# A transformer block on one core: residual and bias put in the output by transfers, a bitwise-or in the search, and the first expert made ready in the context stage

## What is computed

```
xn = (x - mean) / sqrt(var + 1e-5)
q, k, v = split(xn @ W_qkv + b_qkv);  16 heads of 32;  q, k = relu(q), relu(k)
kv_cos = sum over l of (k * cos_l) v;  kv_sin the same with sin_l      (per batch and head)
context = (q cos_l) kv_cos + (q sin_l) kv_sin;  norm the same with the sums of k
attn = (context / (norm + 1e-4)) @ W_out + b_out
probs = softmax(xn @ choice_w.T);  each of 8 experts takes the 1024 rows of a batch with its highest probs
ffn[row] += prob * (silu(xn[row] @ w1[e]) @ w2[e])
out = x + attn + ffn
```

## Time and profile before

| | us |
|---|---|
| median of 3 runs | 2571.82 (2569.92 to 2573.37) |
| the profiled execution | 2573.36 |
| its span in the profile | 2571.6 |
| TensorE busy | 2449.5 (95%) |
| VectorE busy | 1436.1 (56%) |
| GpSimd busy | 1101.0 (43%) |
| ScalarE busy | 664.8 (26%) |
| mean granted clock | 0.98 |

### The profile page before, as it was taken

The page is one execution under the profiler, slowest core; times in us unless marked ns, Lnnn a source line. Parts: engine busy times, 40 slices in busy tenths (PEclk is TensorE's granted clock), DMA queues, the critical chain, the costliest instruction groups (busy, mean ns, idle before and its releaser), DMA issues.

```text
span 2571.6 us, 38730 instructions
## 1 busy us (share of the span) xinstructions
PE 2449.5 (95%) x12990; PEld 2074.7 (81%) x12990; DVE 1436.1 (56%) x3019; ACT 664.8 (26%) x1108; POOL 1101.0 (43%) x938
## 2 busy tenths in 40 slices
PE   6999989999999889769999999999999999999997
PEld 5999978879999878658878878888788788788786
DVE  6666669976666689843444354443534534543443
ACT  3222223322222233222232222322322322322222
POOL 0000015410000055366656566575666666565665
PEclk9999989999999999879999999999999999999999
DMA  5111012321111233243252242433342432522522
GB/s 157 61 37 65 33 43 94 102 90 40 57 49 49 70 113 100 72 101 52 44 115 48 46 112 45 78 81 51 75 83 48 107 52 42 115 48 45 113 45 42
DMA packets 106797, 181.63 MB, mean 71 GB/s; under 512 B 31761, under 2 KB 31761, under 8 KB 106769
## 3 DMA queue, kind: packets, MB, share of 16 engines
q0 software_dynamic: 39552, 68.75, 15.1%
q1 hardware_dynamic: 67216, 112.57, 14.3%
HBM read 112.83 MB, written 68.42 MB: 70 GB/s over the span
## 4 chain that ended last, share of the span: by engine, by line
PE 79%; DVE 12%; issue 4%; DVEq 1%; DMA 1%; POOL 1%; ACT 1%; SPq 1%; POOLq 0%; ACTq 0%
PE ps L1030 26%; PE ps L1031 26%; PE ps L1032 26%; DVE thr L776 2%; DVE work L849 2%; DVE xo L877 1%; DVE k_lo L865 1%; DVE one_lo L916 1%; PE ps L1046 1%; DVE mark L766 1%; DVE w_lo L1003 1%; PE ps L1199 1%; POOL rows L428 1%; DVE rden L853 1%; DVE rden L855 1%
## 5 line engine op out<-in xcount | busy, mean ns | idle before, releaser
L428 POOL DMA_INDIRECT rows<-normed_rows,idx_row x528 | 565.8, 1072 | 207.9 <-issue 206.7
L1030 PE MATMUL ps<-xi_hi,w_hi 128*128 128x512 f32 x1024 | 406.3, 397 | 27.0 <-DVE xi_lo L960 27.0
L1031 PE MATMUL ps<-xi_lo,w_hi 128*128 128x512 f32 x1024 | 400.8, 391 | 0.0
L1030 PE MATMUL ps<-w_hi,h_hi 128*128 128x512 f32 x1024 | 400.2, 391 | 0.0
L1032 PE MATMUL ps<-xi_hi,w_lo 128*128 128x512 f32 x1024 | 399.5, 390 | 0.0
L1032 PE MATMUL ps<-w_hi,h_lo 128*128 128x512 f32 x1024 | 398.8, 389 | 0.0
L1031 PE MATMUL ps<-w_lo,h_hi 128*128 128x512 f32 x1024 | 398.4, 389 | 0.0
L407 POOL TENSOR_TENSOR vv_lo<-qT,vv_hi 128x512 fp32r<-128x512 f32 x64 | 83.4, 1304 | 729.8 <-ACT vv_hi L536 729.7
L997 DVE CAST h_hi<-hf 128x512 fp32r<-128x512 f32 x256 | 111.1, 434 | 441.5 <-ACT hf L580 438.5
L473 POOL DMA_INDIRECT out_dram<-y,idx x128 | 224.6, 1754 | 294.9 <-ACT y L599 278.0
L580 ACT ACTIVATE hf<-ps 128x512 f32<-128x512 f32 x256 | 153.1, 598 | 538.6 <-PE ps L1032 538.6
(11 more groups left out here) (157 smaller groups left out, 4440.9 us busy)
## 6 DMA issues: line engine op xcount, KB each, us to landing
w_raw<-in_L_ffn_w_dram SPq DMA_DIRECT2D x36, 512.0 KB, 8.4
w_raw<-in_L_ffn_w_dram SPq DMA_DIRECT2D x9, 2048.0 KB
xo<-in_L_attn_x_dram SPq DMA_DIRECT2D x34, 512.0 KB, 3.9
normed_rows<-xn SPq DMA_DIRECT2D x34, 512.0 KB, 3.0
xo<-in_L_attn_x_dram SPq DMA_DIRECT2D x64, 256.0 KB, 2.6
out_dram<-xo SPq DMA_DIRECT2D x64, 256.0 KB, 2.0
rows<-normed_rows,idx_row POOLq DMA_INDIRECT x528, 2.6
qT<-in_L_attn_W_qkv_dram SPq DMA_DIRECT2D x3, 1024.0 KB, 8.1
```

Source lines behind the costliest of these rows:

```text
L428: nc.gpsimd.indirect_dma_start(rows[:, tt, a, :], None, pieces[:, :], bass.IndirectOffsetOnAxis(ap=idx_row[:, b, first_tile + tt, a:a + 1] ...
L1030: nc.tensor.matmul(dst, a_hi, b_hi, start=start, stop=False, skip_group_check=True)
L1031: nc.tensor.matmul(dst, a_hi, b_lo, start=False, stop=False, skip_group_check=True)
```

## The change

- **Output.** At the start of each batch GpSimd's queue copies x to the output from DRAM to DRAM, 1024 rows a transfer, and adds the bias by an accumulating transfer from a broadcast tile. In the context stage ScalarE copies the output product to `xo`, and GpSimd stores it with an accumulating transfer. The loads of x, GpSimd's sum, VectorE's sum and SP's stores go.
- **Search.** `settle` multiplies the comparison with the bit's pattern and ors it into the threshold; no predicated copy. The search runs one step earlier: TensorE's count for bit t-1 comes between context products and transposes of step t.
- **Last block of a batch.** Its q products 1 to 3 come behind the last `kv`. In batch 0 the normalised rows of the next batch are turned in step 32 of the context stage; in the last batch nothing is normalised ahead.
- **First expert.** In the context stage of batch 1, list, gather (one transfer a step, steps 11 to 30), transposes, xi, the high part of w1 and half of its remainder are made. w1 is loaded when the projection is done, w2 when the last tile of q is split.
- **Lists in the experts** are made behind up products 4 to 7 in place of 3 to 6.
- **Start.** `choice_w` is loaded by one transfer and transposed by TensorE; w_out is split by GpSimd alone; ScalarE copies q product 0 before the square root.
- The loops over batches and over context steps are written out.

```diff
+            sp.dma_start(ch_rows, choice_w[:, :]).then_inc(ch_in, 16)
...
-                for k in range(KD):
-                    sp.dma_start(ch[:, k, :], choice_w[:, k * P:(k + 1) * P].rearrange("e p -> p e")
-                                 ).then_inc(con_in, 16)
...
+                if b == B - 1:
+
+                    sp.wait_ge(mm_done, AHEAD + B * NBLK * 12)
+                    load_w1(0)
+                    sp.wait_ge(q_ready, B * NT)
+                    load_w2(0)
...
-            pool.wait_ge(w_hi_ready, 4)
+            pool.wait_ge(w_in[O], 16)
+            nc.gpsimd.tensor_copy(wo_hi[:, :, :], raw_weights(O)).then_inc(wo_hi_ready, 1)
+            pool.wait_ge(wo_hi_ready, 1)
...
+            def first_rows(t):
+
+                if t == 10:
+                    for s in range(2):
+                        pool.wait_ge(xn_stored[s], 16 * B * NBLK)
+                    pool.wait_ge(prob_stored, DMA_AHEAD + 16)
+                    pool.wait_ge(idx_ready, AHEAD + 1)
+                    copy_list(0)
+                elif 11 <= t < 27:
+                    gather_piece(0, (t - 11) // HPG, (t - 11) % HPG)
+                elif 27 <= t < 31:
+                    gather_gain(0, t - 27)
...
+                def base_copy(c):
+                    span = slice(b * L + c * BASE, b * L + (c + 1) * BASE)
+                    nc.gpsimd.dma_start(of[span, :], xf[span, :]).then_inc(base_in[c % 2], 16)
+
+                def base_bias(c):
+                    pool.wait_ge(base_in[c % 2], (b * (L // BASE) // 2 + c // 2 + 1) * 16)
+                    span = slice(b * L + c * BASE, b * L + (c + 1) * BASE)
+                    nc.gpsimd.dma_start(of[span, :].rearrange("(t p) d -> p t d", p=P),
+                                        bo[:, :].rearrange("p (t d) -> p t d", t=1).to_broadcast([P, BASE // P, D]),
+                                        accum_op=ALU.add).then_inc(base_ready, 16)
+
+                def add_out(t, ring):
+                    pool.wait_ge(fin, AHEAD + b * NT + t + 1)
+                    nc.gpsimd.dma_start(of[b * L + t * P:b * L + (t + 1) * P, :], xo[:, ring, :],
+                                        accum_op=ALU.add).then_inc(out_stored[ring], 16)
+
+                base_copy(0)
+                for c in range(L // BASE):
+                    if c < L // BASE - 1:
+                        base_copy(c + 1)
+                    base_bias(c)
                 q_lo(0, 0)
...
+                for t in range(NT + 2):
+                    if t < NT - 1:
+                        q_lo(t + 1, (t + 1) % 2)
+                    if t == 2:
+                        pool.wait_ge(base_ready, (b + 1) * (L // BASE) * 16)
+                    if t >= 2:
+                        add_out(t - 2, (t - 2) % RES)
+                    if b == B - 1:
+                        first_rows(t)
...
+                    if t >= 2:
+                        held, uses = (t - 2) % RES, b * (NT // RES) + (t - 2) // RES
+                        act.wait_ge(out_done, AHEAD + b * NT + t - 1)
+                        if uses > 0:
+                            act.wait_ge(out_stored[held], uses * 16)
+                        nc.scalar.copy(xo[:, held, :], ps[:, 5 - par, :]).then_inc(fin, 1)
+                    if b == B - 1:
+                        first_unit(t)
...
-                    me.did(nc.vector.tensor_scalar(hit[:, :], ps[:, 7, 0:2], float(CAP) - 0.5, None, ALU.is_ge))
-                    me.wait()
-                    apart(dve)
-                    me.did(nc.vector.copy_predicated(thr[:, :], hit[:, :], cand[:, :]))
+                    me.did(nc.vector.tensor_scalar(hit[:, :], ps[:, 7, 0:2], float(CAP) - 0.5,
+                                                   bit[:, NT + s:NT + s + 1].bitcast(F32), ALU.is_ge, ALU.mult))
+                    me.wait()
+                    me.did(nc.vector.tensor_tensor(thr[:, :], thr[:, :], hit[:, :], ALU.bitwise_or))
                     me.wait()
...
+            def first_unit(t):
+
+                if t in (16, 20, 24, 28):
+                    rows_turn(0, (t - 16) // 4)
+                elif t in (18, 22, 26, 30):
+                    rows_lo(0, (t - 18) // 4)
+                elif t in (25, 27, 29, 31):
+                    w1_low((t - 25) // 2, (t - 25) // 2 + 1)
...
-                    if first(t, 2):
-                        dve.wait_ge(out_done, AHEAD + b * NT + t - 1)
-                        dve.wait_ge(res_ready, b * NT + t - 1)
-                        held = (ring + 2) % RES
-                        nc.vector.tensor_tensor(xo[:, held, :], ps[:, 4 + par, :], xo[:, held, :],
-                                                ALU.add).then_inc(fin, 1)
...
+                kv(n_last, TPB - 1)
+                pe.wait_ge(v_read, AHEAD + (n_last + 1) * TPB)
+                q_rest(1, 5)
+                pe.wait_ge(lg_read, AHEAD + (n_last + 1) * TPB)
+                q_rest(2, 6)
+                pe.wait_ge(k_read, AHEAD + (n_last + 1) * TPB)
+                q_rest(3, 4)
...
-                        if u % HALVES == 0 and 3 <= m <= 6:
-                            make_list(e * B + (u // HALVES + 1), m - 3)
+                        if u % HALVES == 0 and m >= 4:
+                            make_list(e * B + (u // HALVES + 1), m - 4)
```

More of the change, by code:

```diff
@@ L1051, in _ @@
                 turn_x(0, t, 4 + t)
+                if t == 1:
+                    pe.wait_ge(ch_in, 16)
+                    for k in range(KD):
+                        last = nc.tensor.transpose(ch[:, k, :], ch_rows[:, k * P:(k + 1) * P], ident[0:E, 0:E])
+                    last.then_inc(ch_turned, 1)
             pe.wait_ge(w_ready, 1)
             pe.wait_ge(xT_ready, TPB)
-            with pe.Fori(0, B) as b:
+            for b in range(B):
                 for g in range(G):
@@ L1177, in step @@
-                    if first(t, 1) and not (isinstance(t, int) and t > BITS):
-                        exchange(t)
-                        nc.tensor.matmul(ps[:, 7, 0:2], same_block, cnt[:, 0:2], start=True, stop=True
-                                         ).then_inc(route_pe, 1)
-                pe.wait_ge(sums_ready, b + 1)
-                stage2_steps(pe, step)
-                exchange(BITS + 3)
-                for h in range(2):
-                    last = nc.tensor.transpose(ps[:, 7, h * P:(h + 1) * P], mark[:, h, :], ident)
```

727 lines of the change are left out of this document (388 added, 339 removed).

## The result

The changed kernel takes 2544.51 us (median of 4 runs, 2543.76 to 2547.29) where the kernel before takes 2572.01 in the same comparison (4 runs, 2569.92 to 2573.37): a ratio of 0.9896, 95% interval 0.9879 to 0.9913. The forecast was 2472. The direction was right, the size was 28 us instead of 100, and outside the range.

What follows compares the result with a forecast made beforehand. It took TensorE to bound the experts, VectorE the steady context steps, and waits the entries and first expert. Terms 16.5 + 28.5 + 3 + 42 + 13 + 2 - 5 = 100 us gave 2472 us, range 2452 to 2488.

Steps and rivals of the forecast that it cites:

- Part 7: Projection: copies of x and accumulated bias into the output share engines with x loads; cost 5 us, bounds 0 and 56.
- rival (b): Projection: base transfers hold the loads of x as 4 MB of weights did; 51 us more, 2523; chance 0.12.
- Part 1: Steady context steps: VectorE loses residual sum and select, steps fall from 5.21 to 4.9 us; sum +16.5 us.
- The floor: Steady context step: TensorE's 5.27 us less 0.45 of waiting gives 4.82 us.
- rival (a): Context step does not shorten, the bitwise-or being held beside GpSimd's q remainder; 2490 us; chance 0.17.
- Part 2: Entries of the context stage: moved q products cover the sums and most of the softmax; +28.5 us, bounds 20 and 31.
- Part 3: Between the batches: 13.0 us becomes 11.5; with small stalls +3 us, bounds 0 and 6.
- Part 4: Before the first expert: early preparation leaves 7 us of 49.15 after step 31; +42 us, bounds 36 and 42.5.
- Part 5: Experts: list products one product later end TensorE's waits for one_lo; +13 us, bounds 0 and 14.5.
- Part 6: Start: one load of choice weights, q copied before the square root; +2 us, bounds -3 and +6.
- Rival (c): Context steps: GpSimd's issue of accumulating stores becomes the bound, making the kernel slower; 2597 at 4.25 us an issue; chance 0.04.
- Rival (d): First expert: early preparation does not take hold, giving 20 us instead of 42; 2494 us; chance 0.09.

Runs made afterwards that it cites:

- e1: Changed kernel without the base transfers (copies of x and accumulated bias into the output): ratio 0.9722 to the kernel before.
- e3: Changed kernel with ScalarE's copy and GpSimd's remainder of q made two steps ahead, before the output's work in their queues: ratio 0.9864 to the kernel before.
- e8: Changed kernel with paced base transfers, batch 1's square roots ahead of q copies, and q split two steps ahead: 2472.46 us, ratio 0.9609 to the kernel before.
- e7: Changed kernel with the predicated copy in place of the search's bitwise-or: 2548.34 us, ratio 0.9906 to the kernel before.
- e5: Changed kernel with the first expert's list, gathers, transposes and first weights behind the last context step again: 2566.67 us, ratio 0.998 to the kernel before.
- e4b: Changed kernel with the experts' list products behind up products 3 to 6 again, on the second chip: 2566.34 us, ratio 0.9977 to the kernel before.
- e9: Changed kernel with the bias left out of the output, copies of x issued as in the change: 2538.11 us, ratio 0.9871 to the kernel before.
- e10: Changed kernel with base pieces of 1024 rows, each issued when the next block is normalised, one copy at a time: 2500.03 us, ratio 0.9719.
- e6: Changed kernel with base pieces of 512 rows, each issued when the next block of x is normalised: 2499.60 us, ratio 0.9715 to the kernel before.

## Why the prediction was wrong, step by step

**Part 7** is the step that failed most. "The queues are different ones, so I take 5": the measured cost is 42 to 44 us up to batch 1's step 3 (e1), and the prediction's own sign of being wrong, blocks of over 45 us, stands in the trace with 60.7, 50.4 and 58.7. The upper end, 56, from the load behind 4 MB, was the right row, and rival (b), 51 more, the nearest case; it was given .12. Its terms were wrong too. It charged 7 us to each of eight blocks. In fact six loads took 12 to 17 us and all behind them their usual 4, because the pieces aren't spread over the blocks but issued ahead of them; VectorE stood for four of the six. The length of the traffic was nearly right (80 to 160 us forecast, 75 measured in each batch), but the reasoning went by that total where it should have asked which load is issued while 4 MB are in flight. The argument against (b), "that load stood in the same queue; the base's is another", is refuted: another queue did not protect the loads here. In its place: 18 to 19 us in batch 0, 24 to 25 in batch 1's projection and entry.

**Part 1**: +16.5 forecast, -5.5 measured (+5.1, -10.6). The floor was well placed: 4.94 us a step is reached in e3 and e8, and 4.86 in steps 12 to 17 of the change's batch 1, against 4.9 taken and 4.82 worked out. VectorE's own work of 3.9 us was right as well: its rows add up to 4.94 us a step (batch 0, eight steps from 13 on), of which 0.98 is the bitwise-or's hold. But its share is 89% (130.5 of 146.1 us) where under 80% was the sign. The step that failed is that the select's 0.7 us would go with GpSimd's bias sum. Neither the select's form nor the bias sum was the condition: q's remainder on GpSimd holds the bitwise-or and the predicated copy alike (e7), and the change puts the remainder of q into that very place, behind the accumulating store. That is rival (a), given .17 and priced at one collision a step, 18 us; it cost 16 to 18 (e3), of which 15 in batch 1, where the first expert's preparation stands beside it. For that the forecast charged 1.5 us; e5 measures 14.3.

**Part 2**: in batch 0 12.3 of 12.3. For batch 1, the -18.9 of the table are the base's 24 (e1), the table loads' about 9, and what remains, some +14, for the entry, against 16.2. Right in mechanism, 2 us short in size; the clock at the entries is 1.00 as forecast.

**Part 3**: +0.4 for +3, within 0 to 6. **Part 4**: +40.5 in the gap for +42, bounds 36 and 42.5; the first product is 8.7 us after step 31 for 7. Right, but its price stood in part 1: net, e5 makes it 20.9.

**Part 5**: +21.4 for +13, above its end of 14.5. The waits went as forecast (14.7, and 14.3 in e4b, to none). The term was sized by the wait rows alone, and e4b puts 18.2 us on the stage; the other 3 us of the 21.4 are open.

**Part 6**: +8.1 for +2, but 7.3 of it was given back a block later: the turn of 16.17 us in e1 has no base transfers beside it. TensorE starts its first turn 8.1 us sooner and then stands until the load of x has come, normalised and turned. Net it is 0.8 us, and -1.0 in e1, where the first transposes start at 37.97: within the part's bounds, and below what it forecast.

**Not in the forecast**: ScalarE's table loads, 9 us. Part 6, which moves ScalarE's copy of q ahead of the square root, looked at the start only; the same order in batch 1's loop makes it change tables twice in each block. Rival (c), the store's issue as the bound, is refuted: 0.86 us on GpSimd (median of L446, at most 0.94), where 3.9 would have eaten the gain. The fivefold issue time beside VectorE's work that the Trainium skill gives (SBUF — State Buffer, "A bandwidth-pool intuition that's wrong (but worth ruling out)": 620 ns becoming about 3100) did not appear in any of the 64 stores. Whether VectorE was in a two-port mode beside one of them no trace tells. Rival (d) is refuted by 8.66 us.

The sizes of the errors: part 7 37 us, part 1 22, the table loads 9, part 6's return 7, part 2 2, parts 3 and 4 4; against them parts 5 and 6 with 8 and 6 more than forecast. That is 67 of the 70 us between 100 and 29.8; the same marks in two profiles of the changed kernel differ by up to 3 us, so the rest can't be placed.

## What to carry to other kernels

A bulk transfer is priced by the load that is issued while it is in flight, not by its share of the engines' time: list the loads with a deadline, and issue the bulk right behind the one that is urgent, a piece at a time (here that took 42 to 44 us to almost nothing, with the same bytes, though as many loads came late). When an instruction is long beside another engine's, ask what will stand in that place after the change, not only what leaves it, and whether the chain that the busiest engine waits for runs through it: the same hold cost 16 to 18 us ahead of L1018 and next to nothing behind it. And a reordered queue is to be read in every loop that it runs in: on ScalarE, for the functions that alternate; on GpSimd, for what comes to lie beside VectorE's chain.

## What the runs showed of the hardware

Not expected: a load of 512 KB from SP's queue issued behind 4 MB of copies from DRAM to DRAM on the software queue takes 17.0 us (a bias transfer and a third copy joined them while it stood), with a third and fourth copy close behind 22.6 (e9), against 4.0 alone. The order of issue shows most plainly in e10: the six loads issued 0.65 us behind one copy of 2 MB land 1.1 to 1.2 us after that copy, and the one issued 0.28 us behind it lands in 4.1 us, 5.7 before the copy. e6 has the same with 1 MB: twelve loads land 1.2 to 1.6 us after their copy, and the one issued 0.29 us behind lands in 4.0. The Trainium skill (DMA: Bandwidth & Descriptors, "Queues, rings and completion order") has each DMA engine take the queues in turns, packet by packet; by that a load would come out after about twice its own time, as an estimate some 8 us. The trace doesn't agree (10.2 to 11.2 us behind one copy of 2 MB). Why is open: nothing here tells whether the engines' turns, the copies' packets or the memory behind them hold it. SP's issue of that load is longer as well in most profiles, 2.60 us in e9, but it took its usual 0.40 in the changed kernel's, where the load was as late.

A direct accumulating store of 256 KB costs GpSimd 0.86 us to issue and lands in 4.0 us, cheaper than the indirect one (1.88 us). Where a VectorE and a GpSimd instruction meet, the VectorE one loses here: 160 ns becomes 1133, and 175 becomes 1130 for an addition of 16 numbers a row. GpSimd's remainder loses nothing: 1.28 to 1.33 us in e3 in the 53 of its 64 that hold the addition. Its 1577 ns in the change come from the record's start, 0.26 us ahead of the end of the store's issue (462.12 + 0.85, against 462.71). An activation-table load is 1283 ns, the same in each of 14, and from the end of the copy of q to the start of the square root, with the load between them, it is 1.31 us in six of the seven blocks.
